# Attention probabilities turned by a DMA instead of by TensorE, in 13 of 16 units, and a changed order of GpSimd's weight work

## What is computed

```python
h = grouped_conv(x, conv_weight) + cond @ c_weight.T + bias
q, k, v = rmsnorm(h @ Wq.T), rmsnorm(h @ Wk.T), h @ Wv.T     # q: 32 heads, k and v: 8
scores = einsum('bkgqd,bksd->bkgqs', q, k) / sqrt(128)
attn = softmax(scores + alibi_and_causal_bias)
x = x + einsum('bkgqs,bksd->bkgqd', attn, v) @ Wo.T
x = x + ffn(dynamic_1x1_conv(x, cond))                        # int4 weights, dequantized
```

## Time and profile before

| | us |
|---|---|
| median of 3 runs | 696.57 |
| lowest, highest | 696.26, 696.69 |
| profiled execution, device time | 695.91 |
| profiled execution, first to last instruction | 694.0 |

### The profile page before, as it was taken

The page is one execution under the profiler, slowest core; times in us unless marked ns, Lnnn a source line. Parts: engine busy times, 40 slices in busy tenths (PEclk is TensorE's granted clock), DMA queues, the critical chain, the costliest instruction groups (busy, mean ns, idle before and its releaser), DMA issues.

```text
span 694.0 us, 14580 instructions
## 1 busy us (share of the span) xinstructions
PE 679.3 (98%) x5070; PEld 402.0 (58%) x5070; DVE 549.8 (79%) x828; ACT 424.2 (61%) x1272; POOL 469.0 (68%) x383
## 2 busy tenths in 40 slices
PE   9999999999999999999999999999899999999996
PEld 8766555656656466565665656656535555555553
DVE  4978878879869778886986978687666887888887
ACT  0488483844746566394474747547467777776774
POOL 0468874973876595487377649648536777888885
PEclk9999999999999999999999999999999999999998
DMA  7420365696377278457537637553100000000001
GB/s 256 182 89 1 139 140 121 138 219 90 99 177 179 86 159 217 99 115 232 99 86 191 166 84 152 131 114 75 20 1 1 0 1 1 1 31 32 1 0 61
DMA packets 92752, 69.20 MB, mean 100 GB/s; under 512 B 74752, under 2 KB 75296, under 8 KB 90528
## 3 DMA queue, kind: packets, MB, share of 16 engines
q1 hardware_dynamic: 92272, 68.59, 39.8%
q10 hardware_dynamic: 432, 0.01, 0.0%
HBM read 51.68 MB, written 2.21 MB: 78 GB/s over the span
## 4 chain that ended last, share of the span: by engine, by line
PE 87%; POOL 5%; DVE 4%; issue 2%; ACT 1%; DMA 0%; DVEq 0%; SPq 0%; POOLq 0%; ACTq 0%
PE bank L615 20%; PE bank L616 20%; PE bank L617 20%; PE bank L983 3%; PE bank L984 3%; PE bank L953 3%; PE bank L954 3%; PE bank L667 2%; PE bank L968 2%; PE bank L969 2%; POOL wqlo L1994 2%; PE bank L805 1%; PE bank L762 1%; PE bank L789 1%; PE bank L777 1%
## 5 line engine op out<-in xcount | busy, mean ns | idle before, releaser
L615 PE MATMUL bank<-wohi,oThi 128*128 128x512 f16 x256 | 97.1, 379 | 2.5 <-DVE oTlo L1676 2.3
L615 PE MATMUL bank<-wqhi,cThi 128*128 128x512 f16 x256 | 97.0, 379 | 0.9 <-POOL wqlo L1994 0.6
L616 PE MATMUL bank<-wolo,oThi 128*128 128x512 f16 x256 | 97.0, 379 | 0.0
L617 PE MATMUL bank<-wohi,oTlo 128*128 128x512 f16 x256 | 97.0, 379 | 0.0
L617 PE MATMUL bank<-wqhi,cTlo 128*128 128x512 f16 x256 | 97.0, 379 | 0.0
L616 PE MATMUL bank<-wqlo,cThi 128*128 128x512 f16 x256 | 97.0, 379 | 0.0
L1129 ACT ACTIVATE qraw<-bank 128x512 f32<-128x512 f32 x64 | 37.8, 590 | 78.9 <-PE bank L617 78.3
L1684 DVE SCALAR_TENSOR_TENSOR x<-bank,ysc,x 128x512 f32<-128x512 f32 x64 | 47.7, 748 | 43.9 <-PE bank L617 43.8
L2042 POOL TENSOR_TENSOR qinv<-qms,neghalf 128x8 f32<-128x8 f32 x28 | 53.9, 1924 | 39.4 <-ACT qms L1148 39.4
L1140 ACT ACTIVATE qsq<-qraw 128x128 f32<-128x128 f32 x256 | 75.4, 299 | 1.7
L2004 POOL TENSOR_TENSOR wolo<-wor,wohi 128x512 f16<-128x512 f32 x32 | 39.7, 1261 | 49.2 <-ACT wohi L1109 49.2
(11 more groups left out here) (216 smaller groups left out, 1847.0 us busy)
## 6 DMA issues: line engine op xcount, KB each, us to landing
wqr<-in_wq SPq DMA_DIRECT2D x8, 1024.0 KB, 7.4
wor<-in_wo SPq DMA_DIRECT2D x8, 1024.0 KB, 6.0
raw<-in_gu_w SPq DMA_DIRECT2D x28, 256.0 KB, 3.2
zeros<-in_gu_z SPq DMA_DIRECT2D x28, 256.0 KB, 4.4
wkvr<-in_wkv SPq DMA_DIRECT2D x8, 512.0 KB, 7.2
srow<-in_up_s SPq DMA_DIRECT2D x14, 256.0 KB, 5.2
raw<-in_dn_w SPq DMA_DIRECT2D x14, 256.0 KB, 2.7
zeros<-in_dn_z SPq DMA_DIRECT2D x14, 256.0 KB, 3.8
```

Of the source, the lines that this page charges most:

```text
L615: mm(o, ahi, bhi, start=start and k == 0, stop=False)
L616: mm(o, ahi, blo, start=False, stop=False)
L617: last = mm(o, alo, bhi, start=False, stop=stop and k == n - 1)
```

## The change

For units 2 to 14 the probabilities aren't turned by TensorE. ACT and DVE split `pr` as it lies, query rows on the partitions, into a float16 pair `ppair`, which takes the memory of `sc`. One transposing DMA per unit, issued by SP, turns the pair (128 partitions x 1024 float16, 256 KB) into the new tile `pT`, and TensorE's `apply_probs` waits for its landing (`l_pT`). Units 0, 1 and 15 keep the transposes of TensorE. SP's new `turn_probs` stands behind the up weights and ahead of the down weights. ACT's `probs_high` moves from behind the third query copy to behind the second; DVE's `probs_low` moves ahead of `out_scale` and `gate_ints`. On POOL, in an odd step, the output-weight split no longer stands ahead of `scores_shifted`: one group goes between `query_high(0)` and `probs`, three behind `query_high(1)`.

```diff
+        pT = sb("pT", [P, HQ, 2, P], F16, att)
+        ppair = sc[:, :, :].rearrange("p b k -> p (b k)").bitcast(F16).rearrange("p (t k n) -> p t k n", t=HQ, k=2)
+        def moved_probs(u):
+            return not early_unit(u) and not (isinstance(u, int) and u == UNITS - 1)
@@ SP
+            def turn_probs(u):
+                sp.wait_ge(t_pv, u)
+                sp.wait_ge(d_pTlo, u + 1)
+                sp.dma_start(pT[:, :, :, :].rearrange("p t k n -> p (t k) n"),
+                             ppair.rearrange("p t k n -> p (t k) n"), transpose=True).then_inc(l_pT, 16)
                 load_up(first)
+                if moved_probs(2 * kv - 1):
+                    turn_probs(2 * kv - 1)
                 load_down(first)
...
                 load_up(second)
+                turn_probs(2 * kv)
                 load_down(second)
@@ TensorE
-                pe.wait_ge(d_pTlo, u + 1)
+                if moved_probs(u):
+                    pe.wait_ge(l_pT, 16 * u - 16 * FIRST + 16)
+                else:
+                    pe.wait_ge(d_pTlo, u + 1)
...
-                transpose_probs(u - 1)
+                if not moved_probs(u - 1):
+                    transpose_probs(u - 1)
@@ ScalarE, step
-                queries(u, half, 1)
+                query_copy(u, 1)
+                if moved_probs(u - 1):
+                    probs_high(u - 1)
+                query_squares(u, half, 1)
                 query_copy(u, 2)
-                probs_high(u - 1)
+                if not moved_probs(u - 1):
+                    probs_high(u - 1)
@@ VectorE
+                if moved_probs(u):
+                    V.scalar_tensor_tensor(ppair[:, :, 1, :], pr[:, :, :].rearrange("p (t b) k -> p t (b k)", t=HQ), P_UP,
+                                           ppair[:, :, 0, :], ALU.mult, ALU.subtract).then_inc(d_pTlo, 1)
@@ VectorE, step
                 queries_low(u, 0)
+                if moved_probs(u - 1):
+                    probs_low(u - 1)
                 if half:
                     out_scale()
                 gate_ints(2 * kv - 1 if half else 2 * kv - 2)
@@ GpSimd, probs
-                    pool.wait_ge(t_pT, u)
+                    pool.wait_ge(d_pTlo, u)
@@ GpSimd, step
-                if half:
-                    split_wo(kv, (0, 1))
                 scores_shifted(u - 1)
                 query_high(u, 0)
+                if half:
+                    split_wo(kv, (0,))
                 probs(u - 1)
                 query_high(u, 1)
                 if half:
-                    split_wo(kv, (2, 3))
+                    split_wo(kv, (1, 2, 3))
```

More of the change, by code:

```diff
@@ L231, in build @@
         pr = sb("pr", [P, HB, S], F32, att)
-        pThi = sb("pThi", [P, HQ, G, S], F16, att)
-        pTlo = sb("pTlo", [P, HQ, G, S], F16, att)
+        pT = sb("pT", [P, HQ, 2, P], F16, att)
+        ppair = sc[:, :, :].rearrange("p b k -> p (b k)").bitcast(F16).rearrange("p (t k n) -> p t k n", t=HQ, k=2)
         oThi = sb("oThi", [P, HQ, G, BQ, S], F16, att)
@@ L324, in build @@
         l_qT = sem("l_qT")
+        l_pT = sem("l_pT")
         l_norms = sem("l_norms")
@@ L801, in apply_probs @@
                 for t in range(HQ):
-                    for v, p, k in ((vhi, pThi, 0), (vhi, pTlo, 1), (vlo, pThi, 2)):
+                    for v, p, k in ((vhi, 0, 0), (vhi, 1, 1), (vlo, 0, 2)):
                         for b in range(BQ):
                             keys = slice(S * b, S * b + S)
-                            last = mm(PC[b][:, P * t:P * t + P], v[keys, half, t, :], p[keys, t, :, :],
+                            last = mm(PC[b][:, P * t:P * t + P], v[keys, half, t, :], pT[keys, t, p, :],
                                       start=k == 0, stop=k == 2)
@@ L1223, in probs_high @@
             def probs_high(u):
-                act.wait_ge(t_pT, u + 1)
-                A(pThi[:, :, :, :], prob_bank(u)[:, :].rearrange("p (t g s) -> p t g s", t=HQ, g=G), ACT.Copy,
-                  scale=P_UP).then_inc(a_pThi, 1)
+                if moved_probs(u):
+                    act.wait_ge(p_pr, u + 1)
+                    A(ppair[:, :, 0, :], pr[:, :, :].rearrange("p (t b) k -> p t (b k)", t=HQ), ACT.Copy,
+                      scale=P_UP).then_inc(a_pThi, 1)
+                else:
+                    act.wait_ge(t_pT, min(u, FIRST) + 1)
+                    A(pT[:, :, 0, :], prob_bank(u)[:, :].rearrange("p (t n) -> p t n", t=HQ), ACT.Copy,
+                      scale=P_UP).then_inc(a_pThi, 1)
             def outputs_high(u):
@@ L1669, in probs_low @@
                 dve.wait_ge(a_pThi, u + 1)
-                V.scalar_tensor_tensor(pTlo[:, :, :, :], prob_bank(u)[:, :].rearrange("p (t g s) -> p t g s", t=HQ, g=G), P_UP,
-                                       pThi[:, :, :, :], ALU.mult, ALU.subtract).then_inc(d_pTlo, 1)
+                if moved_probs(u):
+                    V.scalar_tensor_tensor(ppair[:, :, 1, :], pr[:, :, :].rearrange("p (t b) k -> p t (b k)", t=HQ), P_UP,
+                                           ppair[:, :, 0, :], ALU.mult, ALU.subtract).then_inc(d_pTlo, 1)
+                else:
+                    V.scalar_tensor_tensor(pT[:, :, 1, :], prob_bank(u)[:, :].rearrange("p (t n) -> p t n", t=HQ), P_UP,
+                                           pT[:, :, 0, :], ALU.mult, ALU.subtract).then_inc(d_pTlo, 1)
             def outputs_low(u):
@@ L1748, in step @@
                 if half:
-                    probs_low(u - 1)
                     queries_low(u, 1)
```

## The result

The changed kernel takes 713.3 us in the median (710.9 to 716.0, 4 runs) against 696.4 us before (696.2 to 696.7): 2.4% slower, ratio 1.0241, 95% interval [1.0223, 1.0258]. The forecast was 748 us, the range 704 to 772: the direction held and the time lies in the range, but the loss of 17 us is a third of the 52 that were forecast.

A forecast was written before the change was run, and what follows sets the result against it. TensorE was taken as the bound, so any new wait is paid in full. From 695.9 us, +41 of net waits and +10 of clock make 747, put at 748 us with the median's 0.7; range 704 to 772.

The forecast's parts named there:

- The due time, S + 11.65: TensorE reaches apply_probs 11.65 us after S, the start of a step's scores, once the transposes are gone.
- The transposes: Four TensorE transposes per unit, 0.44 us each unit; removing them in thirteen units gains 5.7 us.
- The ready times: Turned pair ready to be sent at S + 9.7 in even steps and S + 10.2 in odd ones.
- DVE's addition: In odd steps, with POOL's weight split gone from beside it, it falls from 1.67 to 0.69 us.
- POOL's instructions: In odd steps one split group, 1.36 us, stands between query_high(0) and probs; about 0.5 us of delay stays.
- The outputs' low halves: On DVE, needed 5 us after the product, whose delay covers them; without that cover an odd step pays about 0.5 us.
- the DMA: Landing of the turned pair: 1.15 setup, 3.6 transfer, 0.65 way back; 5.3 us taken, bounds 2.8 and 6.6.
- wrong if the landing is under 4 us: The prediction's own sign of failure; the other was the wait showing at the scores instead of at the product.
- The new waits of TensorE: In front of the product: 3.3 us in six even steps, 3.8 in seven odd; +41 us net of transposes.
- rival 1: The DMA's size hardly matters, landing at 2.8 us; +9 us, 705 us; chance 0.18 (up to 725).
- The clock: TensorE resting over 3 us per step may lose full clock: 0.8 us for each of 13 waits, +10 us.
- SP's queue: Down weights and query transposes queue behind the turned pair, some 3.9 us of issue; should still arrive in time, no cost.

The follow-up runs named there:

- the tile ahead: Against the changed kernel, the first of four tiles of project_kv is put ahead of apply_probs; 701.2 us, ratio 1.0075 to the kernel before.
- half the tiles: Against the changed kernel, the DMA turns only two of the four query tiles (128 KB), the rest left unturned, for time alone; 703.7 us.
- a part of 32 partitions: Against the changed kernel, the same 256 KB is turned by four DMAs of 32 partitions each in place of one of 128; 771.4 us.

## Why the prediction was right and wrong

**What held.** TensorE was the bound with no slack, so a wait in front of the product is paid in full. The due time, S + 11.65, is 298.49 + 11.65 = 310.14 here, and the recorded idle of 1.45 us before 311.66 starts at 310.21. The transposes were worth 0.44 us each: 28.92 - 0.44 + 1.45 = 29.93 against the measured 30.00. The ready times were right to 0.25 us: issue at S + 10.07 (I took 10.2) and in the even step at 337.96 - 328.49 = S + 9.47 (9.7). DVE's addition fell to 0.69 us. POOL's instructions cost what rows 4 and 5 say, within 0.25 us. The outputs' low halves, which the prediction priced at 0.5 us in an odd step without the cover of the late product, cost 0.7 once the tile ahead took that cover away.

**The step that failed** is the size of one term, the DMA: 5.3 us forecast, 3.1 measured. By its own sign ("wrong if the landing is under 4 us") the prediction is wrong. The new waits of TensorE were to be 3.3 and 3.8 us and were 1.0 and 1.45, 18.5 in all where the forecast has 46; that the time still lies in the range is owed to rival 1, down to which the range was drawn. Two errors made the DMA's size.

The first is mine alone. I read the query transposes as 64 KB; they are 128 KB. The row contradicted me: 129 GB/s for a microsecond is 129 KB, and I explained that away as "counted on both sides". The new DMA is therefore twice theirs, not four times. By the same steps with the right size the landing is 1.15 + 2 x 0.89 + 0.65 = 3.6 us, the waits 1.65 and 2.15, the net 1.2 and 1.7 per step: 7 x 1.7 + 6 x 1.2 = 19 us, 715 us with no clock term. That would have been within 0.3%, in part by luck: this landing is still 0.5 us too long in each of 13 steps, and what the sum leaves out (the late input load, the two early steps and the clock) makes up for most of it.

The second is the pace. 89% of the engines moved 129 KB in 1.0 us, 145 KB in a microsecond at full share; the new DMA moves 262 KB in 1.4 us at 97%, 193 in a microsecond. The number of partitions is not the difference: at full share half the tiles move 131 / 0.65 = 202 KB in a microsecond, and a part of 32 partitions, as many as a query transpose has, 66 / 0.34 = 194. What makes the query transposes slower for their bytes was not tried; the prediction had scaled from the slower kind. The Trainium skill's 261 GB/s ("DMA: Bandwidth & Descriptors", "Latency and other measured facts"), which that page gives for a non-contiguous middle dimension, lay on the other side of the truth: 1.0 us by it, an estimate, 1.4 measured. And SP's issue did not scale at all: 1.25 us for 64 KB and for 256, 1.28 for the 128 KB of a query transpose and 1.20 for half the tiles. I had taken all that exceeds a plain DMA's 0.42 us as going with the amount, from one size; one size cannot tell a fixed part from a growing one.

So rival 1 (the size costs little, 705 us) was the nearest; with 3.1 in place of its 2.8 its sum is 13 x (3.1 - 2.8) = 4 us more, 709, and the rest is the start and a little clock.

**The clock** was given 10 us, 0.8 for each wait as the middle between nothing and 1.6. In the profiled execution it cost next to nothing (0.999), with 11 waits of 0.8 to 1.7 us and two of 1.91 and 2.59. But the two longest of the four runs, 714.9 and 716.0 us, also have the lowest granted clocks, 0.994 and 0.989; they have no profile, so how often the clock fell in them isn't shown. The run with the old order on GpSimd shows two falls, behind waits of 2.57 and 2.13 us that end at 158.75 and 493.78:

```profile
160.00:161.00 1.00, 1.00 (x7) 0.72 (x5) 0.97 (x2) 1.00 (x3) 0.33 (x1) 0.50 1.51 182
...
495.00:496.00 1.00, 1.00 (x6) 0.72 (x5) 0.68 (x2) 1.00 (x3) 1.00 (x2) 0.50 0.85 252
```

Over all profiles the clock fell behind each of 13 rests of 3.9 to 4.6 us, behind some of 2.1 to 2.6 us and not behind others of the same length, and once behind 1.23. Where the clock fell, it cost more than 0.8 us: the step with the 2.57 us took 33.31 us where the changed kernel's, with 2.59 and no fall, took 31.67, a difference of 1.6 us; behind the rests of four parts it cost 1.9 on the mean. The mechanism was real and struck behind shorter waits than the 3 us that the prediction had in mind, but not behind each of them, so 0.8 us for each of 13 waits was too much for the waits that came.

**SP's queue** was put down as harmless. In two early even steps it isn't. In the step that starts at 145.73, DVE waits for the exchanged query norms, which SP issues behind the turned pair; SP issued them 1.2 us before the scores here and 1.8 us before them in the kernel before (start us, us, and in brackets the idle before):

```profile
148.31 0.23 DVE L1667 TENSOR_SCALAR qsc<-qmoved,scale 128x16 f32<-128x16 f32 x1 [1.63 <-DMA qmoved<-norms]
```

That wait was 0.45 us in the kernel before. These two steps take 31.67 and 30.99 us where later even ones take 30.1, 2.5 us together, part of the 18.5. That SP's new order is the cause is argued from these times; no run moves the new DMA in SP's order alone.

**The spread.** Runs of the changed kernel differ by 3.6 and 5 us, those of the one before by 0.5 to 2.4. The profiles of the changed kernel and its variants show two causes, a late input load at the start (1.1 to 2.4 us, in four of them) and a clock that falls behind a rest in some executions. How much each has in a run without a profile stays open, and so does why the load is late.

## What to carry to other kernels

A DMA that takes over work from a saturated engine must land before that engine wants it: sum its setup, transfer and way back against the time left, since 0.44 us of removed work buys no wait of 1 us. Work out the bytes of a neighbouring DMA from its access pattern and check them against the bytes that the trace counts; where the two differ, the pattern was misread until shown otherwise. In a kernel in which four engines follow one another this closely, covering a wait shows the next one a fraction of a microsecond behind it, so the reach of a rearrangement is that fraction, not the wait.

## What the runs showed of the hardware

A transposing DMA is issued in 1.20 to 1.28 us in the median whether it has 64, 128 or 256 KB; it lands after 2.3 us (64 KB, 32 partitions), 2.4 (128 KB, 128 partitions) and 3.1 (256 KB, 128 partitions), so many small ones in a row pay the issue each. The query transposes, 128 KB from 32 partitions, take 2.8 to 3.0 us in the median, 0.4 to 0.6 more than 128 KB from 128 partitions; 32 partitions alone don't explain it, since the parts of 32 partitions kept the engines busy for no more time per byte (194 KB in a microsecond at full share, against 145 for the query transposes); their longer rows and the destination's pattern were not tried. TensorE's granted clock fell from 1.00 to 0.50 behind rests of 1.23, 2.13, 2.28 and 2.57 us in some executions, and did not behind others of 1.23, 2.29 and 2.59; one fall cost 1.6 to 1.9 us.
